# Dealing 49 dense row groups unevenly over six passes of a four-layer graph kernel, with new lengths in its list scheduler

## The reference

```
x = _layernorm(x + _L0_gnn_ref(x, ...))   # hypergraph convolution, twice: x @ W, mean over edges, mean back, PReLU
x = _layernorm(x + _L1_gnn_ref(x, ...))   # GATv2, 8 heads of 32: softmax over the edges of a row, weighted sum
x = _layernorm(x + _L2_gnn_ref(x, ...))   # GAT, 4 heads of 32, then a projection Wp
x = _layernorm(x + _L3_gnn_ref(x, ...))   # GAT, 4 heads of 64, relu, division by the row's norm
```

## Time and profile before

| | us |
|---|---|
| median of 3 runs | 5725.98 (5724.35 to 5736.71) |
| the profiled execution, first to last instruction | 6104.7 |
| pass 0 with the list of edges before it | 0 to 881 |
| pass 1 | 881 to 1644 |
| pass 2 | 1644 to 2130 |
| pass 3 | 2130 to 3175 |
| pass 4 | 3175 to 4244 |
| pass 5 | 4244 to 5130 |
| pass 6 | 5130 to 6105 |

### The profile page before, as it was taken

One profiled execution on the slowest core, in us unless ns is written; L12 is line 12 of the kernel. 1 busy time (PEld: TensorE's weight loads), 2 busy tenths in 40 slices (PEclk: granted clock), 3 DMA queues, 4 the chain that ended last, 5 costly groups with the idle time before them and its releaser, 6 DMA issues. The chain is left out here.

```text
span 6104.7 us, 80176 instructions
## 1 busy us (share of the span) xinstructions
PE 4488.6 (74%) x20170; PEld 3322.8 (54%) x20170; DVE 3734.1 (61%) x10668; ACT 3066.5 (50%) x8955; POOL 3181.6 (52%) x2882
## 2 busy tenths in 40 slices
PE   0243326778988799989968878886999997666664
PEld 0111114555655377777747666765777775444443
DVE  8422212333565277766647778786777775888887
ACT  0132223444577466665535555554444454666666
POOL 1566665554256555454435545453433442677776
PEclk9555558999998599999989989887999998776665
DMA  1476533333246645454534544453444442444442
GB/s 38 151 237 230 197 114 100 115 122 128 99 163 195 222 163 174 172 183 169 177 122 156 164 156 150 153 167 103 145 153 139 154 153 98 133 139 136 141 134 91
DMA packets 360223, 905.86 MB, mean 148 GB/s; under 512 B 69943, under 2 KB 144159, under 8 KB 359770
## 3 DMA queue, kind: packets, MB, share of 16 engines
q1 hardware_dynamic: 249578, 626.47, 29.9%
q0 software_dynamic: 110192, 274.25, 14.8%
HBM read 565.74 MB, written 340.13 MB: 148 GB/s over the span
## 5 line engine op out<-in xcount | busy, mean ns | idle before, releaser
L1063 PE MATMUL psum<-got,sf 128*128 128x256 f32 x1600 | 681.9, 517 | 635.6 <-issue 372.6
L2316 POOL DMA_INDIRECT got<-tab,end_i x600 | 667.9, 1113 | 621.7 <-PE psum L1172 443.0
L2316 POOL DMA_INDIRECT got<-hop,end_i x600 | 629.4, 1049 | 665.2 <-PE psum L1063 403.4
L1063 PEld LDWEIGHTS psum<-got,sf 128*128 128x128 f32 x1600 | 334.6, 240 | 962.4 <-issue 780.3
L1172 PE MATMUL psum<-got,sf 128*128 128x264 f32 (+2 forms) x1200 | 437.3, 453 | 315.1 <-DVE got L2041 178.2
L1321 ACT COPY got<-psum 1x256 f32<-1x256 f32 x796 | 283.6, 356 | 565.3 <-PE psum L1063 228.5
L1967 DVE TENSOR_TENSOR res<-psum,own 128x512 f32<-128x512 f32 x300 | 206.1, 688 | 501.3 <-ACT got L1321 203.5
L1172 PEld LDWEIGHTS psum<-got,sf 128*128 128x128 f32 x1200 | 233.3, 228 | 432.1 <-DVE got L2041 227.4
L1307 ACT CAST sf<-s 128x512 f32<-128x512 uint8 x350 | 214.8, 614 | 452.6 <-DVE s L1956 215.0
L1199 ACT COPY xl_t<-psum 128x512 f32<-128x512 f32 x400 | 231.4, 583 | 312.6 <-PE psum L967 178.5
L1359 ACT ACTIVATE res<-res,l_mo 128x256 f32<-128x256 f32 x600 | 311.0, 589 | 148.2 <-DVE l_mo L1930 145.8
(11 more groups left out here) (511 smaller groups left out, 12956.9 us busy)
## 6 DMA issues: line engine op xcount, KB each, us to landing
own<-hop SPq DMA_DIRECT2D x150, 512.0 KB
x_t<-res SPq DMA_DIRECT2D x150, 512.0 KB
xo<-x_t SPq DMA_DIRECT2D x150, 512.0 KB
hop<-res SPq DMA_DIRECT2D x100, 512.0 KB
tab<-tab SPq DMA_DIRECT2D x50, 536.0 KB
own<-tab SPq DMA_DIRECT2D x50, 536.0 KB
r_t<-rec_b SPq DMA_DIRECT2D x50, 528.0 KB
rec_b<-r_t SPq DMA_DIRECT2D x50, 528.0 KB
```

Of the source, the lines that this page charges most:

```text
L1063: T.matmul(o, sf_of(q)[:, k * P:(k + 1) * P], got_of(q)[:, k * FEAT:(k + 1) * FEAT], start=(p < 3), stop=True).then_inc(at("l_agg"), 1)
L2316: eng.indirect_dma_start(out=dst, out_offset=None, in_=table, in_offset=bass.IndirectOffsetOnAxis(ap=idx, axis=0), bounds_check=rows_ - 1, ...
```

## The change

The 49 dense groups get another gate: of 49 groups, 13 are tied to gathers spread over pass 1, 8 over pass 2, 2 over pass 3, 3 over pass 4, 11 over pass 5 and 12 over pass 6, where before there were about eight in each. `begin[0]` to `begin[12]` are 50, 53, 57 ... 96; then 100, 106, 112, 118, 125, 131, 137, 143; 150, 175; 200, 216, 233; 250, 254, 259 ... 295; and 300, 304 ... 341, 345. Four parts of PE get other lengths in the list scheduler (five numbers).

```diff
+SHARES = (0, 13, 8, 2, 3, 11, 12)
...
+    begin = [p * ng + ng * j // count for p, count in enumerate(SHARES) for j in range(count)]
+    assert len(begin) == nd
...
-        add(("G", "xin", d), 5.2, [spots, ("G", "gather", ng + 6 * ng * d // nd), ("T", "x0", d - 2), ("T", "x1", d - 2)], landing=2.5)
+        add(("G", "xin", d), 5.2, [spots, ("G", "gather", begin[d]), ("T", "x0", d - 2), ("T", "x1", d - 2)], landing=2.5)
...
-                    put(("T", f"wp{h}", q), 1.3, here("Stz"), bank="ring", emptied=here(f"Vwp{h}"))
+                    put(("T", f"wp{h}", q), 1.73, here("Stz"), bank="ring", emptied=here(f"Vwp{h}"))
...
-                    put(("T", f"tab{k}", q), {3: 2.16, 4: 0.93, 5: 0.9}[p], here("Stp0", "Stp1"), bank="ring", emptied=here(f"{te}tab{k}"))
+                    put(("T", f"tab{k}", q), {3: 2.59, 4: 0.93, 5: 0.9}[p], here("Stp0", "Stp1"), bank="ring", emptied=here(f"{te}tab{k}"))
...
-                    put(("T", "lgt", q), 0.87, here("Vzl"), bank="ring", emptied=here("Slgt"))
+                    put(("T", "lgt", q), 1.72, here("Vzl"), bank="ring", emptied=here("Slgt"))
...
-                put(("T", "spr", q), {4: 0.95, 5: 0.82, 6: 1.5}[p], here("Vmax", "Sselm"), bank="ring", emptied=here("Vspr"))
+                put(("T", "spr", q), {4: 1.7, 5: 0.82, 6: 1.0}[p], here("Vmax", "Sselm"), bank="ring", emptied=here("Vspr"))
```

## The result

| | us |
|---|---|
| before, median | 5725.16 (5713.09 to 5736.71, 4 runs) |
| changed, median | 5626.74 (5618.88 to 5629.01, 4 runs) |
| ratio | 0.9827, 95% interval 0.9812 to 0.9843 |

The change makes the kernel 98 us faster.

What follows compares the result with a forecast made beforehand. It took PE to bound passes 3 to 5 and DVE to lead pass 6. Moves of +5 us and lengths of -25 took 6104.7 to 6085 us profiled, scaled to 5707 us (-0.33%), range 5640 to 5782.

Steps and rivals of the forecast that it cites:

- The reading of limits: Whole kernel: PE busy 89%, 83%, 91% of passes 3, 4, 5; DVE leads pass 6 with 79%; pass 2 PE 79%.
- Pass 2, +46: Pass 2: 4.5 more last products at 10.3 us each lengthen it by 46 us (ends 10 and 90).
- Rival 3: Pass 2: gathers again close POOL to dense reads, only 2 groups more done there; 5717 us, chance 0.14.
- Pass 3, -59: Pass 3: 12 groups become 7.5, of which 3.7 save 16 us each, -59 us (ends -38 and -84).
- Pass 4, -77: Pass 4: 3 groups instead of 8, of which 3.5 save 22 us each, -77 us (ends -36 and -82).
- Pass 5, +11: Pass 5: 7.5 last products against 7, +0.5 at 22 us, +11 us (ends 0 and +50).
- pass 6, +84: Pass 6: 15.5 groups against 11, 4.5 more at 18.7 us, +84 us (ends +72 and +122).
- rival 2: End of pass 6: three more groups than counted stand after the last gather, +45 us more; 5749 us, chance 0.20.
- The lengths, -25: New scheduler lengths: a fifth of PE's 128 us idle in pass 4 is misplaced parts, -25 us (ends -80 and +30).
- Rival 1: Pass 4: PE's clock falls to 0.80 with fewer groups, +65 us of link work; 5768 us, chance 0.15.
- The other rule: Passes 3 and 5: by weight-load share (72%, 75%) PE has room, groups cost nearer pass 2's price, moves about +20 us.
- Rival 4: Pass 4: the lengths matter more and it loses most of its stalls, -80 instead of -25; 5656 us, chance 0.18.

Runs made afterwards that it cites:

- the second trace: The kernel before, unchanged, profiled once more: span 5721.8 us, passes 0 and 1 at 612 and 614 us.
- the first trace: The kernel before, unchanged, as first profiled for the prediction, a disturbed execution: span 6104.7 us.
- the best arrangement: Against the kernel before: gates 13, 8, 2, 3, 15, 8, passes 3 and 4 gated at 153, 178, 241, 243, 246, only tab's pass 3 length new: 0.9661, 5524 us.

## Why the prediction was wrong

**Where the sum went wrong.** In a profiled execution the forecast was -20 us and the second trace gives -105. By pass, with the -25 of the lengths counted in pass 4 where the forecast sized it:

| pass | forecast | measured |
|---|---|---|
| 0 and 1 | 0 | -5 |
| 2 | +46 | +59 |
| 3 | -59 | -159 |
| 4, with the lengths | -102 | -107 |
| 5 | +11 | +5 |
| 6 | +84 | +101 |

The step that failed is the term of pass 3: it had too few groups leaving and gave the length of `tab` nothing of its own. Passes 2 and 6 together went 30 us the other way. Pass 4 came out near only by luck, as shown below.

**The reading of limits** held for passes 3 to 6: PE is fullest in 5, then 3, then 4, and DVE leads in 6, in the second trace too. Pass 2 has PE at 85% there, not 79%. What was misread is the first trace: the 378.7 us over the median were taken as an even stretch of 6.6%. Against the second trace 72 and 149 us lay in passes 0 and 1, 52 in pass 2 and 108 in the rest. Pass 2 was taken at 486 us and is 434.

**Pass 2, +46.** The step "some 18 groups read before the end of pass 2 instead of 13" failed. The 13 left out the four groups read from 2100 us on the earlier trace rows, still before 2130: before the change 17 are read by then (6 in pass 1, 11 in pass 2), and after it 21. 18 last products ran in pass 2, not 14.5. The indirect reads of line 2316 in pass 2 of the kernel before, and of the same line (now 2320) in the changed one:

```profile
L2316 POOL DMA_INDIRECT x_in<-in_x,didx x44: 994/999/1520, 1453.9 to 1851.7; - x44
L2320 POOL DMA_INDIRECT x_in<-in_x,didx x60: 994/999/1671, 1450.5 to 1840.9; - x60
```

Four are one group: 15 were read instead of 11. Before, the last four groups come in a heap after 1825 us; after, none do. POOL was busy 339 of 493 us and had gaps for the reads, but it had such gaps before too (287 of 434), and it waited less for hops than before (32 us against 52). Why the new order has the reads between the gathers is not shown. Rival 3, a smaller gain in reads, fell with it. The price was taken too high: 59 us for 8 groups, 7.4 each, where 10.3 was taken. The stretch that gave the 10.3 held a wait of 42.5 us of the first gathers for the tables of pass 1, which stands once in pass 2 of every one of these traces, and it was all put on the dense groups. The clock was 0.98 in the whole pass, from 0.81.

**Pass 3, -59.** It gave -159. Two terms failed. The count was 10 groups fewer, not 4.5: 8 were done in pass 2 already, and pass 3 ends with 21 done, not 23, since two groups that have been read stay unfinished until the next are. (With no dense read in passes 3 and 4, gates 13, 8, 0, 0, 14, 14, two groups read in pass 2 finish only in pass 5.) And it held 43 us of the length of `tab`, which the prediction had put under "in this number" with the lengths and sized by pass 4. The price of 16 looks right on average (159 / 10) by luck: with the gates alone it is 119 / 10, or 12, and it is not one price, but 7 a group from 12 to 7 and 16 from 7 to 2, and below two groups the pass got longer.

**Pass 4, -77.** It gave -107 with the lengths and -126 without them, 25 a group: the groups were priced too low and the lengths had the wrong sign here, and the two errors cancel. The ends of the price, 10.3 and 23.4, left out what it is: the highest end was the PE time of a group over PE's share, on the view that a pass can't be delayed by more than its fullest engine is used. One group in the middle of an even stretch cost 37 us, and eight cost 31 each, where the PE time was put at 20.1. The idle 128 us of PE were read as misplaced lengths (-25). In the undisturbed stretch PE is idle 1.3 us a link group, which would be 57 us over these 45; so about 70 of the 128 came with the dense groups.

**Pass 5, +11, and pass 6, +84.** +5 and +101. Pass 6 got 6 groups, not 4.5, at 16.8; 18.7 had been taken. After the last gather 144 us remain with four last products, against 107 with two:

```profile
5472.00:5616.00 144.00, 81.35 (x301) 58.25 (x300) 99.27 (x357) 95.50 (x346) 68.42 (x62) 0.73 0.18 61
```

so the pile-up of rival 2 is there, but in a smaller size and inside that sum.

**The lengths, -25.** Alone they gave 15: right in size, though 30 came from pass 4 and 18 went in pass 5. With the gates, tab's gave some 45 (0.9918 to 0.9832; 43 in pass 3). The rest came to nothing: with them pass 4 is about 20 us longer (943 against 922), and passes 5 and 6 are some 25 us shorter.

**Rival 1**, the clock of pass 4: it stayed at 0.88 with three groups spread and rose to 0.92 with none. The rule that stood against the emptied pass (the Trainium skill, TensorE: Matmul & The Clock Gate, section Part 1: The HAM clock gate) had nothing to act on, for PE got busier in it, not idler (86% of 805 us, from 83%). The other rule (the Trainium skill, Perfetto Trace Analysis, section Identifying the Most-Contended Engine), by which passes 3 and 5 have room, would have made the moves +20 us; they were -47, so for the sum it pointed the wrong way, though the first five groups out of pass 3 did have about pass 2's price (7 us). **Rival 4** had the right sign and not the place: pass 4 lost its stalls through missing dense groups.

The sum failed as a whole because it priced a group by the busy time of the fullest engine and called the moves a zero sum. The range was too narrow above all for pass 3, where the count and the order changed together.

## What to carry to other kernels

Where work that depends on nothing fills the gaps of a tight dependent chain in a fixed order, its price is not its busy time: take the chain's bare period (14.6 us a link group in pass 4 here), count what one filler adds to it (37 us for 20 to 25 of PE), and put fillers where a pass runs slow for another reason (7 to 10 us in pass 2) or at its end, if a run shows that it pays there (18 us a group in pass 4, but a loss in pass 3). Correct a scheduler's lengths one at a time and time each with the arrangement that it will be used with: one of five was worth some 45 us here, and the other four together cost about 69 us in the best arrangement (0.9661 to 0.9781) and nothing in that of the change. And profile the unchanged kernel again when its span is well over its median.

## What was not expected of the hardware

In pass 2 the granted clock rose from 0.50 to 1.00 when dense work filled the waits of the hops; 15 link groups took 105 us bare, and ten took 99 us with dense work between them, PE busy 94. Kernel before, then changed:

```profile
1707.00:1812.00 105.00, 72.07 (x120) 29.67 (x119) 20.36 (x30) 52.80 (x135) 59.72 (x60) 0.50 0.73 233
1726.00:1825.00 99.00, 94.05 (x409) 70.08 (x408) 74.04 (x215) 89.13 (x291) 64.40 (x64) 1.00 0.60 198
```

That is 2.9 us more for a link group, with 6.9 us of dense PE work in each (94.05 less the hops' 24.6, over ten). The hops themselves, in the same order:

```profile
L1063 PE MATMUL psum<-got,sf 128*128 128x256 f32 x120 | 72.4, 707 | 33.4 <-ACT got L1321 33.4
L1067 PE MATMUL psum<-got,sf 128*128 128x256 f32 x80 | 24.6, 389 | 4.7 <-ACT got L1325 4.7
```

PE is busy with them 4.8 us a link group at 0.50 and 2.5 at 1.00, so the clock gives back 2.3 us a group on the chain that the dense work lengthens. How the rest of the cheapness is shared, no run separates. Also open is why the nearer lengths of `lgt` and `spr` give the worse order in pass 4.
